# Cross attention, four layers: each batch's values times Wo taken from one product formed ahead for all batches, instead of values and then a projection

## What is computed

```python
# layers 0 and 2 ("wide"): 16 heads of 64, context projected by Wk, Wv (1024 x 1024)
q, k, v = x @ Wq, ctx @ Wk, ctx @ Wv
probs = softmax(q k^T * 64**-0.5 + col_bias)      # per head, 512 x 77
x = (probs v, heads side by side) @ Wo + bo + x   # Wo: 1024 x 512
# layers 1 and 3 ("narrow"): 16 query heads of 32, 4 key/value heads
xn = rmsnorm(x) * w
q, k, v = xn @ wq, ctx @ wk, ctx @ wv
x = (softmax(q k^T * 32**-0.5) v) @ wo + x        # wo: 512 x 512
```

## Time and profile before

| | us |
|---|---|
| median of 3 runs | 2066.46 (2065.11 to 2067.47) |
| the profiled execution | 2066.7 |
| its span, first to last instruction | 2064.9 |
| PE busy | 2024.2 (98%) |
| DVE, ACT, POOL busy | 1398.2 (68%), 966.0 (47%), 649.5 (31%) |
| context part, up to the first scores | 267.6 |
| first wide layer, first narrow, second wide, second narrow (start of the scores of units 0, 32, 64, 96) | 514.5, 365.9, 532.5, 384.4 |

### The profile page before, as it was taken

How to read it: one execution, slowest core, us unless ns; L and a number is a source line. 1 busy time by engine, 2 the same in 40 slices (tenths; PEclk the granted TensorE clock), 3 DMA queues, 4 the chain that set the end, 5 groups by cost and what they waited for, 6 DMA issues and landing times.

```text
span 2064.9 us, 31181 instructions
## 1 busy us (share of the span) xinstructions
PE 2024.2 (98%) x11482; PEld 1760.5 (85%) x11482; DVE 1398.2 (68%) x2408; ACT 966.0 (47%) x1814; POOL 649.5 (31%) x534
## 2 busy tenths in 40 slices
PE   8999999999999998999999999999999989999998
PEld 8999988888888887788888888888888877888887
DVE  5332365775577557788888676557755775888886
ACT  3222354544355354555555454345443553555553
POOL 1000043311232244454444431223122543444441
PEclk9999999999999999999999999999999999999999
DMA  7889742222122222343333332222221222333332
GB/s 196 183 176 200 191 97 67 68 65 79 51 72 71 70 71 74 89 107 100 87 98 94 101 96 68 72 60 67 66 79 52 72 77 81 74 92 92 88 72 84
DMA packets 262537, 191.02 MB, mean 93 GB/s; under 512 B 197522, under 2 KB 199986, under 8 KB 259826
## 3 DMA queue, kind: packets, MB, share of 16 engines
q1 hardware_dynamic: 262386, 189.03, 35.7%
HBM read 132.66 MB, written 56.26 MB: 91 GB/s over the span
## 4 chain that ended last, share of the span: by engine, by line
PE 48%; issue 30%; POOL 11%; DVE 6%; ACT 2%; DMA 1%; SPq 1%; POOLq 0%; DVEq 0%; ACTq 0%
PE acc_bank L877 6%; POOL prob L1311 6%; PE acc_bank L261 4%; PE t_bank L857 4%; PE acc_bank L263 4%; PE acc_bank L262 4%; PE q_bank L835 4%; PE q_bank L837 3%; PE q_bank L839 3%; PE ctx_bank L261 3%; PE ctx_bank L262 3%; PE ctx_bank L263 3%; POOL x_s L1286 3%; PE s_bank L261 2%; POOL rest L1320 2%
## 5 line engine op out<-in xcount | busy, mean ns | idle before, releaser
L1311 POOL TENSOR_TENSOR prob<-prob,rinv 128x1232 f32<-128x1232 f32 x128 | 288.3, 2252 | 1006.3 <-DVE rinv L1195 1006.2
L1053 ACT ACTIVATE q_s<-q_bank 128x512 fp32r<-128x512 f32 x192 | 114.7, 597 | 489.3 <-PE q_bank L839 486.2
L877 PE MATMUL acc_bank<-pT_s,vals_s 128*128 128x512 f32 x1024 | 337.8, 415 | 0.0
L835 PE MATMUL q_bank<-x_s,w_s 128*128 128x512 f32 x768 | 319.4, 416 | 0.0
L1153 DVE TENSOR_REDUCE mx<-s_bank 128x4 f32<-128x308 f32 x512 | 240.1, 469 | 108.6 <-PE s_bank L801 54.3
L837 PE MATMUL q_bank<-x_s,w_s 128*128 128x512 f32 x768 | 313.3, 408 | 0.0
L839 PE MATMUL q_bank<-x_s,w_s 128*128 128x512 f32 x768 | 313.1, 408 | 0.0
L261 PE MATMUL acc_bank<-o_s,w_s 128*128 128x512 f32 x752 | 300.4, 400 | 2.8 <-DVE o_s L1186 2.5
L263 PE MATMUL acc_bank<-o_s,w_s 128*128 128x512 f32 x752 | 293.6, 390 | 0.0
L262 PE MATMUL acc_bank<-o_s,w_s 128*128 128x512 f32 x752 | 293.1, 390 | 0.0
L1044 ACT ACTIVATE prob<-prob,rstd 128x308 f32<-128x308 f32 x256 | 140.7, 553 | 263.2 <-DVE prob L1157 238.0
(11 more groups left out here) (107 smaller groups left out, 4092.8 us busy)
## 6 DMA issues: line engine op xcount, KB each, us to landing
stream<-x_back SPq DMA_DIRECT2D x128, 256.0 KB, 2.6
x_front<-stream SPq DMA_DIRECT2D x96, 256.0 KB, 3.3
x_back<-stream SPq DMA_DIRECT2D x96, 256.0 KB, 4.0
kvw_raw<-kvw SPq DMA_DIRECT2D x17, 1024.0 KB, 8.4
k_scr<-k_out SPq DMA_DIRECT2D x36, 308.0 KB, 10.5
keys_s<-k_scr SPq DMA_DIRECT2D x128, 77.0 KB, 2.5
v_scr<-v_out SPq DMA_DIRECT2D x8, 1024.0 KB
vals_s<-v_scr SPq DMA_DIRECT2D x512, 6.5 KB
```

The source lines that it names most:

```text
L835: pe.matmul(out, w[0], x_now[0], start=k == 0, stop=False)
L877: mm = pe.matmul(out, w, pT_s[:, part], start=i == mine[0] and part == 2 * n and w is v[0], stop=i == mine[-1] and w is terms[-1][0] and p ...
L1311: pool.tensor_tensor(view, view, rinv[:, slot].unsqueeze(2).broadcast_to([P, TILES * GH, CTX]), ALU.mult).then_inc(p_norm, 1)
```

## The change

1. **Context part.** In rounds 0 to 7 the values are formed transposed (`vt`, four chains of 96 matmuls in all with 308 columns, where 120 with 256 stood), and between the chain steps of the next round `outputs` multiplies the values of each of the 4 heads of the group by that head's 64 rows of Wo: 5 blocks of rows x 4 heads x 2 matmuls of 512 columns. High part and rest of the values lie above one another in the 128 rows, so two matmuls do. The product V Wo of all batches (616 rows x 4 heads x 512) is not split; ACT and DVE copy it from PSUM, and it is stored to `vw_scr` in rows of 8 KB through a ring of three 1 MB buffers (`staged`). Wo is loaded each round (`wo_raw`) and split. Keys are stored in whole rows of 616.
2. **Wide steps.** `project` and the splitting of the values go. Two units at a time (a pair: 616 probability columns, five blocks of 128, 128, 128, 128 and 104) are multiplied by their rows of V Wo straight into the four output chunks of the batch: 4 x 5 x 3 = 60 matmuls a pair, two chunks a step (`wide_values`), in steps u+3 and u+4. `add_wide` adds each to the residual, twice as often as `add_result` did. The rows are loaded at the head of each SP step (`load_rows`, twelve DMAs), split by ACT (`split_rows`) and POOL (`rest_rows`).
3. **Rest transposes.** Both kinds: the rest columns of two units are gathered by POOL side by side and turned once a pair, in the odd unit's step. So a unit has 10 transposes in the mean, not 12. In the narrow layers the values of an even unit must wait for this and end behind the projection of their step (`behind`), and their bank is read at the head of the next step.
4. `WEIGHTS` no longer streams Wo of the wide layers, and the narrow ones' weights come earlier.

The diff, cut to its core:

```diff
-        for j in range(NJ):
-            pe.wait_ge(w_lo[1], j + 1)
-            for r in range(NV):
-                values(r, j)
+            for i in outs_after(j, step):
+                r, h = divmod(i, GH)
+                if i == 0:
+                    pe.wait_ge(vt_lo, 4 * j)
+                    pe.wait_ge(wo_lo, j)
+                before = OUTS * (j - 1) + i - 4
+                if before >= 0:
+                    pe.wait_ge(vw_dve if i % 2 else vw_act, before // 2 + 1)
+                out = banks[4 + i % 4][0:VROWS[r], :]
+                v = vt[(j - 1) % 2][:, h, r * P:r * P + VROWS[r]]
+                pe.matmul(out, v, wd[:, 0, 512 * h:512 * h + 512], start=True, stop=False)
+                pe.matmul(out, v, wd[:, 1, 512 * h:512 * h + 512], start=False, stop=True).then_inc(vw_mm, 1)
...
+        for j in range(NJ):
+                    for k in range(KC):
+                        chain_step(0, n, k)
+                        outputs(j, step)
+                        step += 1
...
+        u = (s - 3) // 2 * 2
+        if not 0 <= u < NU or kind(u).name == "B":
+            return []
+        return [(u, 2 * (s - 3 - u) + i) for i in range(2)]
...
+        if u % 2 == 0:
+            return 0, 1
+        return (0, 1, TWICE) if kind(u).name == "A" else (0, TWICE, 1)
...
+                u, m = plan.wide(s)[0]
+                half, b, p = plan.chunk(u, m) // 2, u // GROUPS % B, u // (2 * UNITS)
+                if half >= 2:
+                    sp.wait_ge(rows_lo, 2 * half - 2)
...
+                into = rows_s[:, half % 2]
+                for e in range(2):
+                    src = vw_scr[4 * p + (u + e) % GROUPS].rearrange("r (h c) -> r h c", h=GH)
+                    for h, t0, t1, n, row in WIDE_PIECES:
+                        block, row = (2 * e + n, row) if n < 2 else (4, row + REST * e)
+                        sp.dma_start(into[row:row + t1 - t0, block],
+                                     src[CTX * b + t0:CTX * b + t1, h, P * m:P * (m + 2)])\
+                          .then_inc(rows_loaded[half % 2], 16)
...
-                    mine = [i for i, (_, o) in enumerate(kind(u).blocks) if o == m]
-                        terms = [(v[0], 2 * n), (v[0], 2 * n + 1), (v[1], 2 * n)]
-                        if n == TWICE:
-                            terms = [(v[0], 2 * n + m)] if kind(u).name == "A" else [(v[0], 2 * n), (v[1], 2 * n)]
-                        for w, part in terms:
-                            mm = pe.matmul(out, w, pT_s[:, part], start=i == mine[0] and part == 2 * n and w is v[0],
-                                           stop=i == mine[-1] and w is terms[-1][0] and part == terms[-1][1])
...
+                for u, m in plan.wide(s):
+                    n, item = plan.chunk(u, m), plan.acc[("pv", u, m)]
+                    after(pe, acc_out, item - 1)
+                    pe.wait_ge(rows_lo, n + 1)
+                    out = acc_bank[item % 2][:, :]
+                    for block in range(BLOCKS):
+                        if m == 0:
+                            pe.wait_ge(t_lo, wide_turn(u, block) + 1)
+                        rows, p = BROWS[block], wide_block(u, block)
+                        w = [ring(n)[0:rows, h, block] for h in range(2)]
+                        pe.matmul(out, w[0], p[0:rows, 0], start=block == 0, stop=False)
+                        yield
+                        pe.matmul(out, w[0], p[0:rows, 1], start=False, stop=False)
+                        yield
+                        mm = pe.matmul(out, w[1], p[0:rows, 0], start=False, stop=block == BLOCKS - 1)
+                        if block == BLOCKS - 1:
+                            mm.then_inc(acc_mm, 1)
...
-                    beside(scores(s, 2), v, 4)
-                    turned(0)
-                    beside(scores(s, 3), v, 4)
-                    turned(1)
-                    turned(2)
-                    for gb, m in plan.projections(s):
-                        project(gb, m)
+                    run(wide, 6)
+                    run(v, 6 if behind else 8)
+                    beside(scores(s, 0), wide, 12)
+                    beside(scores(s, 1), wide, 12)
+                    beside(scores(s, 2), q, half)
+                    if not behind:
+                        projected(projections)
+                    turned(turns[:2])
+                    beside(scores(s, 3), q, half)
+                    turned(turns[2:])
+                    if behind:
+                        projected(projections[:1])
+                        run(v, 2)
+                        projected(projections[1:])
...
-                    run(v, 3)
-                    turned(0)
-                    run(q, half)
-                    run(v, 9)
+                    run(wide, 30)
+                    run(v, 3)
+                    turned(turns[:1])
+                    run(q, half)
+                    run(v, 3 if behind else 5)
+                    turned(turns[1:2])
+                    if plan.stats_at(s) is not None:
+                        stats(plan.stats_at(s))
+                    turned(turns[2:])
+                    if behind:
+                        projected(projections[:1])
+                        run(v, 2)
+                        projected(projections[1:])
+                    else:
+                        projected(projections)
...
+                act.wait_ge(rows_loaded[n // 2 % 2], 32 * len(WIDE_PIECES) * (n // 4 + 1))
+                if n >= CHUNKS:
+                    act.wait_ge(acc_mm, plan.chunk_ended(n - CHUNKS))
+                act.activation(ring(n)[:, 0], raw_rows(n), ACT.Copy).then_inc(rows_hi, 1)
...
+                dve.wait_ge(acc_mm, plan.ended[("pv", u, m)])
+                if u % GROUPS == 0:
+                    dve.wait_ge(back_loaded[m], 16 * (gb + 1))
+                    dve.scalar_tensor_tensor(out=here, in0=out, scalar=bo[:, p, m:m + 1], in1=here,
+                                             op0=ALU.add, op1=ALU.add).then_inc(acc_out, 1)
+                else:
+                    dve.wait_ge(acc_out, plan.acc[("pv", u - 2, m)] + 1)
+                    dve.tensor_tensor(here, out, here, ALU.add).then_inc(acc_out, 1)
...
-                        for t in range(TILES):
-                            tile_scores(s, t)
+                    for t in range(TILES):
+                        if s < NU:
+                            tile_scores(s, t)
+                        if t == 0 and plan.split_values(s - 3):
+                            rest_o(s - 3)
...
-                    for copy in range(2):
-                        ins = pool.tensor_copy(twice[:, :, :, copy], ends)
-                    ins.then_inc(p_gathered, 1)
+                size = REST if kind(u).name == "A" else REST_B
+                pool.tensor_copy(rest[:, :, size * slot:size * slot + size], prob[:, slot, :, SC - size:SC])\
+                    .then_inc(p_gathered, 1)
+            def rest_rows(n):
+                pool.wait_ge(rows_hi, n + 1)
+                pool.tensor_tensor(ring(n)[:, 1], raw_rows(n), ring(n)[:, 0].bitcast(F32), ALU.subtract).then_inc(rows_lo, 1)
...
+                if s % (2 * UNITS) != 1:
+                    load_rows(s + 2)
+                if s % (2 * UNITS) == 1:
+                    load_rows(s + 2)
```

914 lines of the change are left out of this document (541 added, 373 removed).

## The result

The changed kernel takes 2138.4 us (median of 4 runs, 2137.4 to 2140.3) against 2067.0 for the kernel before (2065.1 to 2067.7), a ratio of 1.035, with a 95% interval of 1.033 to 1.037. That is 71.4 us slower, where 35 were forecast: the direction was right, the forecast had half of the size, and the time lies outside its range of 2067 to 2124. The profiled execution spans 2135.3 us, 70.4 more than the one of before.

The account below looks back on a forecast made before the run. The prediction took PE to bound the kernel. From 2066.7 us it added +14.6 of matmuls and +20.6 of waits, giving 2101.9, or 2101.7 against the median, with a range of 2067 to 2124.

Parts of the forecast that it names:

- the walk of the context rounds: Context part: nothing waits in rounds 1 to 7; the tightest split ends some 3 us into the next round, before 3.8.
- part (b) of the starts of wide layers: Narrow to wide, steps 64 to 66: scores with nothing beside them wait for subtraction, bias, queries and sums, 6 us.
- the changeovers: Wide to narrow, from unit 32 and again near unit 96: V Wo matmuls fill part of the idle time, -9 us.
- the matmuls: Whole kernel: context +68.4, wide steps -39.8, narrow steps -14.0, together +14.6 us.
- the odd narrow step: Odd narrow steps: reading the even unit's values between tiles 0 and 1 delays scores 3 by 0.60 us, +15.6 in all.
- the last round: Last context round: products set closer and first loads of x split ahead of the copies, +3 us.
- part (a): Starts of wide layers: first rows reach ACT 11 us into step 2, delaying the bias of score tile 3, 5 us.
- (1): Rival: the changeovers heal entirely, the lost 33 us go and no other new wait shows, 2048 us; chance 0.09.
- (2): Rival: half of (1) is had and the narrow wait shows in part, 2069 us, the same; chance 0.09.
- (3): Rival: context rounds wait for their stores, 40 us a round instead of 36, +32, 2133 us; chance 0.13.
- (4): Rival: in wide steps DVE and POOL shut each other out, 0.8 us over PE 58 times, 2148 us; chance 0.03.
- (5): Rival: the narrow wait does not show since PE is late there anyway, 2086 us; chance 0.66 together with the forecast.

Follow-up runs that it names:

- experiment 5: The new kernel with the second of the two matmuls of each V times Wo product left out in the context rounds: 2107.5 us.
- experiments 6 and 11: The new kernel with narrow turns per unit and set-up behind drains: 2105.3 us; with the edits of Experiment 1, Experiment 2 and Experiment 3 together: 2107.7 us.
- experiment 7: The kernel before, with VectorE's late addition of a projection moved between score tiles 0 and 1 in the narrow steps: 2098.6 us.
- Experiment 1: The new kernel with VectorE's 39 set-up instructions moved behind the drains of context rounds 0 and 1, seven at a time: 2129.0 us.
- Experiment 2: The new kernel with the residual's reload issued ahead of the keys on SyncE, in step 66 alone: 2132.1 us.
- Experiment 3: The new kernel with VectorE's rest of the held-back values moved behind score tile 1 in 26 odd narrow steps: 2129.6 us.
- experiment 4: The new kernel with each narrow unit turning its own rest columns again, wide layers still sharing; some wide output uses overwritten numbers: 2116.2 us.
- Experiment 10: The kernel before, with score tiles 0 and 1 of the first two narrow units moved earlier in VectorE's order at both wide-to-narrow changeovers: 2070.4 us.
- experiment 8: The new kernel with SyncE issuing the loads of whole rows last in each wide step, not first: 2258.4 us.

## Why the prediction was right, and where it failed

The forecast was wrong by 36.7 us, and nearly all of that is in the waits: +56.4 us where its sum had +20.6. The steps that failed are the walk of the context rounds, which left out round 0 (12 us too little), part (b) of the starts of wide layers (13), the even narrow steps, taken as free of waits (7), and the changeovers, which gained less (3.5).

**Right: the matmuls**, +14.4 us for +14.6 (both by the cadences of before, so this says that they were counted rightly), and that most of their time is on the path where PE is full (experiment 5: 37 us of matmuls out, 31 us of time). The design itself costs time: V times Wo adds more matmuls in the context part than it takes from the wide layers. Even with its waits mended the kernel stays 39 to 40 us behind (experiments 6 and 11). Right too were the odd narrow step (0.66 us for 0.60, and 0.60 again in experiment 7), the last round (the same chain, about 5 us for 3), and the late rows of part (a) in step 2 (2.8 us in unit 2 for 5).

**Failed: "Nothing waits in rounds 1 to 7", as the whole of the context part.** The sentence held for its rounds; but the walk began with round 1. In round 0 the new bank layout meets VectorE's set-up chain, 11 us of this part's 12 us error. The chain was in the trace of before, in plain sight, costing nothing: there it was work without a reader. Experiment 1 shows it.

**Failed: "starts of wide layers", part (b).** 6 us against 18.9. I walked scores 2 and the queries, but not VectorE's last addition, whose input is reloaded by a queue that stands behind the keys. In one place of the text I had priced a late reload, "some 0.5 us a batch"; its real place was the one step where the residual is wanted a step later than elsewhere. Experiment 2 shows 7.9 us of the 13. The waits of scores that I had at 1.2, 1.0, 1.4 and 2.6 us were right (1.2, 1.2, 1.3 and 2.4 above their cadences). Most of the remaining 5 us are the half-clock spell of 6.8 us in step 66 (2.8), which I had not counted, and the values that wait in front of unit 65 while unit 62's held-back values are read (1.6).

**Failed in size: narrow steps.** The odd term stood; the even step was left at zero. The shared block is drained by two instructions for one, and ends where it is needed: 0.28 us in each even step. Experiment 3 leaves these 0.28 us, experiment 4 takes all but 0.08.

**Changeovers: right in sign, -5.5 for -9.** The walk had 1.2 us for unit 34, and it waits 2.8, 2.3 of them for the shared block; in the four times that PE waits for this block there it loses 9.4 us (experiment 4 gives back 6.3 us at the changeovers). Experiment 10 adds that the order of VectorE tried there buys none of the 18 us that a changeover loses before.

**The rivals.** (1) and (2) fell with the above. (3) did not come: the context part moves 252 GB/s with a DMA share of 0.74 where it had 188 and 0.87, and the 1 MB loads land in 5.9 us for 8.4:

```profile
kvw_raw<-kvw SPq DMA_DIRECT2D x17, 1024.0 KB, 5.9
```

(4) did not come either. GpSimd's new instruction is there 128 times, and VectorE's query split keeps its mean (672 ns, 671 before):

```profile
L1605 POOL TENSOR_TENSOR o_s<-rows_s,o_s 128x640 fp32r<-128x640 f32 x128 | 199.2, 1568 | 65.3 <-ACT o_s L1328 65.3
...
L1426 DVE TENSOR_TENSOR q_s<-q_bank,q_s 128x512 fp32r<-128x512 f32 x192 | 129.0, 672 | 28.6 <-ACT q_s L1297 12.5
```

The Trainium skill, "SBUF — State Buffer", has in the section "SBUF: two separate sides" a narrower rule than the one I took from its Terms: only a VectorE instruction with two inputs in SBUF, or in a two-port mode, competes with GpSimd. These read one input from a bank, and the trace agrees with that; what an instruction with two inputs in SBUF would lose no run here shows. (5), the narrow wait that does not show, fell with the odd steps' 0.66 us and experiment 7.

**A wrong number.** I had SyncE's issues for the rows at 0.61 us each; they take 0.37 (24 in 8.82 us). So ScalarE has the first rows 8.1 us into step 2, not 11, which is part of why (a) cost 2.8 us and not 5.

## What to carry to other kernels

When a change lets a new user into banks or buffers, walk it from the first round: whatever the draining engine did there unpunished (set-up, one-time work) now has a reader. When a result is held back by a step, follow it across the end of its loop, its reload and the queue of that reload included; steady steps tell nothing about that. And an instruction put between two tiles of an engine on which PE waits can cost nearly its full length in every step (here 0.60 of 0.68 us), more than the 0.44 us of matmuls that the narrow sharing saved in two steps.

## What the runs showed that I had not expected

A half-clock spell costs only what PE runs in it. In the 9.6 us stand the granted clock fell to half (1.2 GHz) for 10.2 us, and this cost 1.4 us, since PE stood in the first 7.3. Spells of 3.4 us came and went at the end and at the second changeover with edits hundreds of us away (experiments 1 and 2), worth 1.5 us each time. Only one execution of each kernel is traced, and the four of experiment 2 lie 5.9 us apart, with mean clocks of 0.990 to 0.994; so differences of that size between two traces need no cause in the code that was edited.

A queue's order can be free in most steps and cost 108 us in 14 others (experiment 8, half-clock spells included): the rows' place behind the staged weights is harmless until a step has a weight to stage.
